# Third convolution: one run of 64 weighing matmuls per chunk, with folding, node sums and spread placed behind the gathers

## What is computed

```python
h = jax.nn.elu(spline_conv(h, row, col, basis, idx, stn2_w, stn2_b))
h = jax.nn.elu(h @ stn3_w + stn3_b)
t = h @ stn4_w + stn4_b
new_pseudo = jnp.clip(pseudo + t[col] - t[row], 0.0, 1.0)
basis2, idx2 = spline_basis(new_pseudo)
return spline_conv(x, row, col, basis2, idx2, conv_w, conv_b)
```

## Time and profile before

| | us |
|---|---|
| median of three executions | 10374.85 (10366.98 to 10381.05) |
| profiled execution | 10362.97 |
| its span, first to last instruction | 10361.0 |
| third convolution, chunks 0 to 147 | about 6480 to 8415 of the span |

### The profile page before, as it was taken

One profiled execution on the slowest core, in us unless ns is written; L12 is line 12 of the kernel. 1 busy time (PEld: TensorE's weight loads), 2 busy tenths in 40 slices (PEclk: granted clock), 3 DMA queues, 4 the chain that ended last, 5 costly groups with the idle time before them and its releaser, 6 DMA issues. The chain is left out here.

```text
span 10361.0 us, 393328 instructions
## 1 busy us (share of the span) xinstructions
PE 7407.7 (71%) x147710; PEld 6528.2 (63%) x147711; DVE 7530.9 (73%) x18535; ACT 4644.2 (45%) x12114; POOL 5944.5 (57%) x5974
## 2 busy tenths in 40 slices
PE   5465555554773656565658995899999978888888
PEld 4455555554563555555557884777777757777776
DVE  7688888886774444445456883888888869999887
ACT  0011111110552333333335662444454459999997
POOL 0477777776334777777776770777777731111111
PEclk6555555555555878787879996999999989989888
DMA  1222233332102333333333221222222225555554
GB/s 45 36 82 74 74 74 76 74 75 49 25 8 67 112 114 108 115 111 116 114 110 96 75 76 27 62 63 62 63 63 61 63 67 142 142 142 142 140 139 99
DMA packets 850875, 875.93 MB, mean 85 GB/s; under 512 B 629325, under 2 KB 632837, under 8 KB 850286
## 3 DMA queue, kind: packets, MB, share of 16 engines
q1 hardware_dynamic: 623150, 526.57, 18.4%
q0 software_dynamic: 227648, 348.32, 13.1%
HBM read 631.28 MB, written 135.27 MB: 74 GB/s over the span
## 5 line engine op out<-in xcount | busy, mean ns | idle before, releaser
L1573 ACT ACTIVATE c_products<-c_pa 125x512 f32<-125x512 f32 x2368 | 1222.7, 603 | 1786.1 <-PE c_pa L1617 1770.2
L1448 POOL DMA_INDIRECT c_near_ranked<-h_rows,c_idx x1568 | 1656.4, 1056 | 477.7 <-issue 477.4
L786 POOL DMA_INDIRECT edges_by_rank<-rank_stage,rank_idx x1568 | 1607.1, 1025 | 502.7 <-issue 466.4
L1900 POOL DMA_INDIRECT edges_b<-c_send_rows,c_send_idx x1184 | 1316.6, 1112 | 397.4 <-issue 357.5
L1617 PE MATMUL c_pa<-c_near_apart,c_basis 32*125 32x128 f32 x18944 | 743.5, 294 | 1006.3 <-DVE c_near_apart L1536 904.3
L1617 PEld LDWEIGHTS c_pa<-c_near_apart,c_basis 32*125 32x125 f32 x18944 | 636.6, 195 | 1124.9 <-issue 1124.9
L1628 PE MATMUL c_py<-c_products,c_weights 125*64 125x128 f32 x18944 | 1212.4, 283 | 0.0
L2413 POOL DMA_DIRECT2D rows<-local_rows x548 | 294.7, 538 | 1586.1 <-DVE hot_d L2431 1438.4
L295 PE MATMUL acc_s<-hot_col,hot_row 128*123 128x91 f16 x3136 | 421.2, 312 | 990.7 <-ACT start_table L741 795.8
L1628 PEld LDWEIGHTS c_py<-c_products,c_weights 125*64 125x64 f32 x18944 | 1069.0, 141 | 58.0 <-issue 0.2
L2059 ACT ACTIVATE c_products<-c_pa 125x256 f32<-125x256 f32 x2368 | 710.8, 384 | 787.7 <-PE c_pa L2142 787.7
(11 more groups left out here) (410 smaller groups left out, 18864.6 us busy)
## 6 DMA issues: line engine op xcount, KB each, us to landing
rows<-local_rows POOLq DMA_DIRECT2D x548, 256.0 KB, 4.0
own_d<-hparts SPq DMA_DIRECT2D x2192, 48.0 KB, 3.0
hi_rows_in<-hi_rows SPq DMA_DIRECT2D x392, 256.0 KB
c_dst_rows_in<-dst_rows SPq DMA_DIRECT2D x148, 512.0 KB
near_by_rank<-c_near_ranked SPq DMA_DIRECT2D x98, 768.0 KB, 5.0
rows_both<-hi_rows SPq DMA_DIRECT2D x196, 196.0 KB
near_h<-c_near_h SPq DMA_DIRECT2D x74, 512.0 KB
c_near<-near_h SPq DMA_DIRECT2D x148, 256.0 KB
```

The lines of the kernel that those rows point to most:

```text
L786: pool.indirect_dma_start(g.ranked, bass.IndirectOffsetOnAxis(idx[:, r, q:q + 1], 0), stage[:, r, q, :], None, bounds_check=last_rank, oob ...
L1448: pool.indirect_dma_start(near[:, b, q, :], None, g.h1_rows, bass.IndirectOffsetOnAxis(idx[:, b, q:q + 1], 0), bounds_check=last_node, oob ...
L1573: last = act.activation(by_round[:, half, r, rnd], pa[0:K3, r, 0:TR * P].rearrange("p (f e) -> p f e", f=width), ACT.Copy)
L1900: pool.indirect_dma_start(g.edges_b, bass.IndirectOffsetOnAxis(sending.idx[:, n, q:q + 1], 0), sending.rows[:, n, q, :], None, bounds_chec ...
```

## The change

`weigh` loses its round: all 32 features are weighed in one run in the fourth round, behind the outer products. In every round the gather follows the outer products (in the fourth the weighing stands between), and `fold_out` and `node_sums` follow the gather. `spread` goes from behind the third gather to behind the fourth, and `take_own` from behind the third `choose` to behind the fourth. The whole diff:

```diff
@@ in third_conv, block.vector, chunk
                     make_outer(k + 2, half, 1)
                 if left >= 3:
                     choose(k + 3, 1 - half, 2)
-                    take_own(k + 3)
                 if left >= 2:
                     make_basis(k + 2, half, i + 2, 1)
                 if left >= 3:
                     choose(k + 3, 1 - half, 3)
+                    take_own(k + 3)
                     move(k + 3, 1 - half)
@@ in third_conv, block.tensor
-            def weigh(k, half, rnd):
-                if rnd == 0:
-                    pe.wait_ge(s_kept, k * ROUNDS + (ROUNDS + 1))
-                    pe.sem_inc(s_pe_turn, 1)
-                for f in range(rnd * F // ROUNDS, (rnd + 1) * F // ROUNDS):
+            def weigh(k, half):
+                pe.wait_ge(s_kept, k * ROUNDS + (ROUNDS + 1))
+                pe.sem_inc(s_pe_turn, 1)
+                for f in range(F):
                     n = f % KP
                     last = pe.matmul(py[n * F:(n + 1) * F, 0:P], weights[:, f, :], outer[:, half, f, :],
                                      start=(f < KP), stop=(f >= F - KP))
-                if rnd == ROUNDS - 1:
-                    last.then_inc(s_used, 1)
+                last.then_inc(s_used, 1)
@@ in third_conv, block.tensor, chunk
                 for rnd in range(ROUNDS):
                     if left >= 1:
                         outer_products(k + 1, 1 - half, rnd)
+                    if rnd == ROUNDS - 1:
+                        weigh(k, half)
+                    if left >= 3:
+                        gather(k + 3, 1 - half, rnd)
                     if rnd == 0 and not first:
                         fold_out(k - 1, k + 4 if left >= 2 else NCK + 1)
                     if rnd == 1 and not first:
                         node_sums(k - 1)
-                    weigh(k, half, rnd)
-                    if left >= 3:
-                        gather(k + 3, 1 - half, rnd)
-                        if rnd == 2:
-                            spread(k + 3)
+                    if rnd == ROUNDS - 1 and left >= 3:
+                        spread(k + 3)
```

## The result

The changed kernel takes 10394.28 us (median of 14 executions, 10381.67 to 10422.18) where the kernel before, on the same chips, takes 10371.74 (10366.98 to 10391.03). The ratio is 1.0021, with a 95% interval of 1.0013 to 1.003. So the change costs 0.2%; the forecast was a gain of 0.37%, and the time lies above the range. The prediction is wrong.

The account below looks back on a forecast made before the run. VectorE with one detour over TensorE was taken to set 13.08 us a chunk. Going to 12.80 saves 0.28 over 144 chunks, -40 us, plus 2 for the tail: -38 on 10374.85 gives 10337 us, range 10311 to 10380.

Parts of the forecast that it names:

- The rival that said so: POOL's nine indirect DMAs a chunk set the pace, staying at 13.08 us; gain nothing, 10373 us; chance 0.14.
- the unstretched 11.6: POOL's queue for one chunk if VectorE's instructions did not lengthen its DMAs: 11.6 us and a little for the index copy.
- The run of 64 to the gather: TensorE's weighing in the fourth round, up to the gather behind it: 1.88 us against 2.32 in quarters; bounds 1.7 and 2.32.
- The ring: Loop from fourth gather through choose, reduction, hats, second keep, outer rounds and weighing to the next fourth gather: 12.80 us.
- gather start to choose start: From TensorE's start of the fourth gather to VectorE's start of the fourth choose: 1.15 us.
- VectorE alone: VectorE's own work, without the detour over TensorE, sets the pace: 12.53 us a chunk, 10298 us; chance 0.05.
- The tail: Last chunks of the stage, where weighing no longer covers keeps and the last fold waits: 2 us lost.
- own_wide's on TensorE: TensorE's wait for VectorE's own_wide before spread, 0.78 us a chunk, would go.
- the outer round's on VectorE: VectorE's wait for the fourth round of outer products before the second half of the basis, 0.55 us a chunk, would go.
- the keeps': TensorE's waits for ScalarE's keep before the second, third and fourth outer rounds would grow from 0.47 to over 1 us.
- the one before choose: VectorE would newly wait for the gather before the fourth choose, some 0.3 us or more a chunk.
- The rival of a run that isn't cheaper: Weighing 64 in one run still takes 2.32 us, making chunks 13.24 us: +25 us, 10400 us; chance 0.11 (or longer ring).

Follow-up runs that it names:

- the last experiments: Index copy for own_shift made by VectorE instead of POOL: on the kernel before, 10374.25 us; on the kernel before with only spread and take_own moved, 10262.73 us.
- its control: The kernel before with the eighth send of every chunk of the third convolution left out: 10387.71 us, ratio 0.9997.
- seven sends: The changed kernel with the eighth send of every chunk of the third convolution left out: 10328.37 us, ratio 0.9945 against before.
- the copy moved: The changed kernel with the index copy for own_shift made by VectorE instead of POOL: 10331.93 us, ratio 0.9947 against before.
- the half of the change without it: The kernel before with only spread and take_own moved behind the fourth gather and choose, weighing in quarters: 10406.51 us, ratio 1.0018.
- the fastest kernel: The kernel before with spread and take_own moved, weighing in quarters, and the index copy made by VectorE: 10262.73 us, ratio 0.9879.
- one half alone: The changed kernel with spread and take_own back in their old places, weighing in one run, gathers ahead of folding: 10557.93 us, ratio 1.0164 against before.
- the split basis: The changed kernel with the instruction for half a basis split in two of half the length: 10336.77 us, ratio 0.9951 against before.

## Why the prediction was wrong

**The step that failed** is the overlap with POOL: the forecast took it that POOL's queue would fit into 12.80 us a chunk, and the runs showed a POOL chunk of 13.28. The rival that said so had the mechanism, its sign in the profile (VectorE waits before own_wide for a DMA) and the point from which it decides (a POOL chunk over 12.80 us) as they happened; it was given 0.14 and the forecast 0.70. The prediction had the number in hand: it said that POOL stands still for nothing but its issue gaps, so that POOL needed its full 13.08 us at the present pattern. It then took the unstretched 11.6 as what POOL could do, and counted on fewer collisions for the rest, which no row supported. The change touches nothing of POOL's, so fewer or shorter meetings alone had to give 0.28 us; they came out 0.20 longer. That meetings can give as much is true (13.02 against 12.3 us for one POOL program in the last experiments), but no row of before said which way they would go.

**The price of that rival** was wrong as well. Slack used up, the gain is nothing, 10373 us: parity. Measured is +0.20 us a chunk, 144 x 0.20 = 29, against 27.3 in the stage. The sum took POOL's durations as fixed; they depend on where VectorE's long instructions stand, and VectorE's place is now given by POOL's own landing. What was missing was a bound above zero for POOL's own stretch.

**The terms of the forecast** held, once POOL was out of the way. The run of 64 to the gather: 1.88 us, as reckoned; it lasts 1.95 by its record. take_own doesn't wait for spread: choose to reduction 0.52 for 0.53. The ring: 12.70 us for 12.80. Against its control the chunk step is 12.83 - 13.19 = -0.36, for -0.28. The 0.10 by which the ring is shorter lies in one term, gather start to choose start: 7211.00 - 7209.95 = 1.05 for 1.15, which had been read in the last chunks. VectorE alone: 12.3 us for 12.53. What the 0.2 are made of stays open: the instruction for the node sums takes 352 ns for 466, but dst_hots' long one, twice a chunk, 790 for 746. The tail: +3.2 for +2. One bound was worked out wrongly: a slope 10% lower gives a run of 1.75 us, not 1.7.

**The waits forecast** came as told in part: own_wide's on TensorE and the outer round's on VectorE are gone, the keeps' grew from 0.47 to 244.5 / 128 = 1.91 us a chunk (over 1 was forecast), and the one before choose came in full only where POOL was relieved (62.8 us in 122 chunks with seven sends, 79.0 in 124 with the copy moved).

**The rival of a run that isn't cheaper** forecast slower too, at 10400. That this is near the measured time is chance, for its reason isn't there: the run isn't over 2.2 us, and the half of the change without it is as slow.

**The page of the Trainium skill**, "SBUF — State Buffer", section "Who interferes with whom" (whichever of VectorE's two-input and GpSimd's instruction comes later is fully blocked): the traces agree on the blocking, 1.76 us for 0.98. From it I had worked out that a faster VectorE holds POOL as often in less time. The runs don't bear that out. By what the mean send has above 0.98 us, eight sends are held 1.06 us a chunk at 13.08 us, 1.22 at the slower 13.28, and only 0.43 at 12.3, where of 1041 sends none lasts 1.5 us or more. How long two streams hold each other depends on how they are in step, not on their speeds alone: before, 91 of the 244 sends that begin inside the basis do so in its first 0.4 us; in the fastest kernel none of 260 does, and the earliest begins 0.70 us into it.

## What to carry to other kernels

An engine whose busy time and issue gaps fill the period may have no slack to give, even if nobody waits for it: before crediting a gain, ask whether each engine's queue, at its present durations, fits the new period, and what would shorten those durations. That an engine is full doesn't make it the bound, nor is its present queue time what it needs; who waits for it, and how far ahead its results are, tells the first, and a run with its work cut tells both. And test the halves of a combined change apart: here one half alone cost 1.6%, the other cost 0.2%, and the other with a small copy moved off POOL gained 1.2%.

## What the hardware showed unexpectedly

- POOL's index copy of 128x4 takes 223 ns before and 516 ns after, the same instruction; in after with seven sends it takes 223 again, with the split basis 224. It stretches like the sends, by what VectorE does beside it: before, all 31 copies of 6600 to 8200 us begin beside the short instructions for the positions, and after, 25 of 30 begin inside the basis.
- POOL falls into step with VectorE. Its queue, added up as above, fills the chunk in four kernels of different pace: 13.08 before, 13.28 after, 8 x (1.105 + 0.305) + 1.102 + 0.305 = 12.69 with the copy moved, 8 x (1.034 + 0.305) + 1.278 + 0.305 = 12.29 in the fastest, while VectorE waits for it in only one of the four. In the fastest kernel own_shift is issued between 4.8 and 5.2 us ahead of its own_wide in every chunk of 6600 to 8200 us, and before between 5.4 and 7.9: well over the 2.5 that are needed, and yet POOL doesn't run further ahead. That its collisions regulate it, more of them when it is ahead, fits this but was not tried.
- The holding up goes both ways. VectorE's long instruction in dst_hots lasts 0.73 us at least and 0.98 at most. It lasts over 0.8 in 3 of 246 cases before, 53 of 240 after and 65 of 261 in the fastest kernel, and all of these but one began while one of POOL's DMAs was running.
- The granted TensorE clock is 0.97 in 7000 to 7200 us of after, for 1.00 before and in the fastest kernel; TensorE had longer waits there (up to 2.0 us). TensorE isn't in the chain from POOL to own_wide, so by this reading the clock isn't what lengthened the chunk; no run separates the two.
